# Block rows gathered by token in a routed vision tower, and the second T5 layer's feed-forward split between its units and the choice of experts

## The reference

```python
h = tokens(x)
h = h + spiking_attention(layernorm(h));  h = h + moe8_linear(layernorm(h))       # top 2 of 8
h = h + quant_attention(layernorm(h));    h = h + t5_encoder(layernorm(h))        # 4 layers
h = h + rope_attention(layernorm(h));     h = h + moe16(layernorm(h))             # top 2 of 16
h = h + prope_attention(layernorm(h));    h = h + moe_mixed(layernorm(h))         # top 8 of 16

# t5_encoder, layers 0 to 3: x = x + attn(rms(x)); then layers 0 and 2:
x = x + relu(rms(x) @ wi) @ wo                       # 192 -> 768 -> 192
# and layers 1 and 3 a mixture on y = rms(x):
vals, idx = top_k(y @ gate, 2)                       # 8 experts
x = x + relu(y @ wi) @ wo + sum_e cw_e * gelu(y @ w1_e) @ w2_e
```

## Time and profile before

| | |
|---|---|
| median of 3 runs | 1727.51 us (1727.13 to 1731.24) |
| profiled execution | 1732.31 us, its span 1730.4 us |
| PE busy | 1401.0 us, 81% of the span |
| PEld busy | 1101.9 us, 64% |
| DVE busy | 644.4 us, 37% |
| ACT busy | 467.7 us, 27% |
| POOL busy | 464.5 us, 27% |

### The profile page before, as it was taken

One profiled execution on the slowest core, in us unless ns is written; L12 is line 12 of the kernel. 1 busy time (PEld: TensorE's weight loads), 2 busy tenths in 40 slices (PEclk: granted clock), 3 DMA queues, 4 the chain that ended last, 5 costly groups with the idle time before them and its releaser, 6 DMA issues. The chain is left out here.

```text
span 1730.4 us, 35498 instructions
## 1 busy us (share of the span) xinstructions
PE 1401.0 (81%) x14426; PEld 1101.9 (64%) x14426; DVE 644.4 (37%) x1668; ACT 467.7 (27%) x1226; POOL 464.5 (27%) x597
## 2 busy tenths in 40 slices
PE   6468855999998799599998899668339995876998
PEld 6164433888875798488876589526329993453756
DVE  2445663433432122333342222355511124543424
ACT  0420242443442111243343111123103331422120
POOL 0010273322333243232232424224043441320000
PEclk9688865999998899799999899886559997857999
DMA  5010203100003432600000453240043552020000
GB/s 125 0 29 13 87 1 123 37 2 2 2 3 140 149 114 84 191 2 2 3 2 2 168 183 117 82 118 5 1 171 122 178 187 79 4 57 0 28 27 19
DMA packets 56096, 115.08 MB, mean 67 GB/s; under 512 B 16384, under 2 KB 43268, under 8 KB 50848
## 3 DMA queue, kind: packets, MB, share of 16 engines
q1 hardware_dynamic: 38848, 58.02, 11.3%
q0 software_dynamic: 17088, 54.81, 9.1%
HBM read 137.97 MB, written 24.87 MB: 94 GB/s over the span
## 5 line engine op out<-in xcount | busy, mean ns | idle before, releaser
L1296 PE MATMUL bank<-xT,w 96*128 96x512 f32 x192 | 86.2, 608 | 15.5 <-ACTq L1350 15.5
L1149 PE MATMUL bank<-t_ew,t_hg 128*128 128x192 f32 x552 | 97.2, 327 | 0.0
L1389 DVE SCALAR_TENSOR_TENSOR h<-bank,cw,h 128x192 f32<-128x192 f32 x128 | 53.5, 418 | 99.8 <-PE bank L1312 82.9
L1035 POOL DMA_INDIRECT t_ew<-in_t_moe,source x46 | 48.0, 1043 | 154.8 <-DVE t_og L1217 124.9
L1149 PEld LDWEIGHTS bank<-t_ew,t_hg 128*128 128x128 f32 x552 | 88.7, 190 | 0.2
L329 PE MATMUL bank<-ident,rows 128*96 128x128 f32 x112 | 25.4, 419 | 76.9 <-DVE rows L312 76.9
L1181 ACT ACTIVATE t_hg<-bank 128x384 f32<-128x384 f32 x92 | 40.1, 488 | 168.2 <-PE bank L1137 131.7
L1177 ACT ACTIVATE l_hg<-bank,l_ew 128x128 f32<-128x128 f32 x186 | 51.4, 375 | 122.6 <-PE bank L1137 82.4
L1296 PEld LDWEIGHTS bank<-xT,w 96*128 96x128 f32 x192 | 37.3, 196 | 60.3 <-issue 43.8
L1704 PE MATMUL bank<-t_wo,t_ctx 128*128 128x192 f32 x384 | 75.0, 348 | 0.5 <-ACT t_ctx L1798 0.4
L1133 PE MATMUL bank<-t_xgT,t_ew 128*128 128x128 f32 x552 | 70.8, 279 | 3.8 <-DVE t_xgT L1208 3.3
(11 more groups left out here) (329 smaller groups left out, 3028.3 us busy)
## 6 DMA issues: line engine op xcount, KB each, us to landing
rows_in<-blank SPq DMA_DIRECT2D x2, 2967.0 KB
...
```

What stands on the lines that cost most here:

```text
L1035: pool.indirect_dma_start(k.ew[i % W_SLOTS][:, 0:weights.shape[1]], None, weights, bass.IndirectOffsetOnAxis(ap=k.source[:, b:b + 1], axis=0),
L1149: mm = pe.matmul(k.bank[6 + b % 2][:, 0:DIM], k.hg[b % 2][:, m, :], w[:, SPLIT + m * DIM:SPLIT + (m + 1) * DIM], start=(m == 0), stop=(m = ...
L1296: mm = pe.matmul(k.bank[(u * FC + m) % 4][:], k.w1[s][:, c, m * P:(m + 1) * P], k.xT[:, c, n * HALF:(n + 1) * HALF], start=(c == 0), stop= ...
L1389: ins = dve.scalar_tensor_tensor(out, src, k.cw[:, tile, bass.ds(col, 1)], out, ALU.mult, ALU.add)
```

## The change

- The normed tokens are written to `rows_in` in their own order, by SP, one tile as soon as it is normed: in `t5_pair_phase`, and in `norm_phase` before the 16 experts (`keep`). The two extra columns, `clear_rows` and `send_rows` are gone.
- `plan_blocks` splits each token's place into block and slot, and makes from them 16 one-hot tiles (`hots`) and value tiles (`vals`), which PE multiplies (`list_places`) into a list: which token fills each slot of each block. `keep_list` turns that into `token` (what to gather) and `dest` (where the result goes). Rows are then gathered from `rows_in` by indirect DMAs from POOL (`fetch_rows`), into four slots instead of three; the first four in `fetch_first`, which now also stands in the router phase of the 16 experts.
- The two best experts are picked by two maxima (`choose_two`) instead of a comparison of all pairs; `weigh_two` makes the weights from one Exp of the difference. Top 8 keeps the comparison.
- In `t5_pair_phase` the second layer's units of tiles 0 to 3 do their feed-forward in their steps (w = 8 to 11, `fed` = 12); `t5_choice_phase` is left with tiles 4 to 7.
- The last feed-forward's first layer is split in 128 rows and two halves of 64 rows instead of 96 and 96, and its norm and router with it.

```diff
-X_SLOTS, W_SLOTS, O_SLOTS = 3, 4, 3
-ROW = DIM + REST + 2
-C_TOKEN, C_SECOND = DIM + REST, DIM + REST + 1
+X_SLOTS, W_SLOTS, O_SLOTS = 4, 4, 3
+ROW = DIM + REST
 EXPERT = SPLIT + FC * DIM
...
+            if keep:
+                for t in range(NT):
+                    sp.wait_ge(k.normed, t + 1)
+                    sp.wait_ge(k.doubled, t + 1)
+                    sp.dma_start(k.rows_in[t * P:(t + 1) * P, :], k.rows[:, t, :]).then_inc(k.sent, 16)
+                sp.wait_ge(k.sent, 16 * NT)
...
+                fetch_first(pool, k, nb, sparse)
...
+def choose_two(k, dve, link, n_e, norm, sparse):
+    each = [P, NT, n_e]
+    lg, ex, rest = k.logits[:, :, 0:n_e], k.ex[:, :, 0:n_e], k.cw[:, :, 0:n_e]
+    favour = k.favour[:, 0:n_e].unsqueeze(1).broadcast_to(each)
+    def pick(src, c):
+        best, early, hit = k.red[:, c, :], k.red[:, 4 + c, :], k.picked[:, c, :, 0:n_e]
+        link(dve.tensor_reduce(best, src, AX_X, ALU.max))
+        link(dve.tensor_tensor(hit, src, best.unsqueeze(2).broadcast_to(each), ALU.is_equal))
+        link(dve.tensor_tensor(hit, hit, favour, ALU.mult))
+        link(dve.tensor_reduce(early, hit, AX_X, ALU.max))
+        link(dve.tensor_tensor(k.sel[:, c, :, 0:n_e], hit, early.unsqueeze(2).broadcast_to(each), ALU.is_equal))
+    pick(lg, 0)
+    link(dve.scalar_tensor_tensor(rest, k.sel[:, 0, :, 0:n_e], -BIG, lg, ALU.mult, ALU.add))
+    pick(rest, 1)
     if sparse:
-        dve.wait_ge(k.normed, 1)
-        for c in range(2):
-            link(dve.tensor_tensor(k.picked[:, c, :, 0:n_e], k.sel[:, c, :, 0:n_e], cw, ALU.mult))
-            link(dve.tensor_reduce(k.gate[:, c, :], k.picked[:, c, :, 0:n_e], AX_X, ALU.add))
+        dve.tensor_tensor(k.selb[:, 0:NT * n_e].rearrange("p (t e) -> p t e", e=n_e), k.sel[:, 0, :, 0:n_e],
+                          k.sel[:, 1, :, 0:n_e], ALU.add).then_inc(k.chosen, 1)
+    if norm != "top":
+        link(dve.tensor_tensor(ex, lg, k.red[:, 0, :].unsqueeze(2).broadcast_to(each), ALU.subtract))
+    dve.tensor_tensor(k.gate[:, 1, :], k.red[:, 1, :], k.red[:, 0, :], ALU.subtract).then_inc(k.std_in, 1)
...
+def list_places(pe, k, nb, bank):
+    for i in range(2 * NT):
+        pe.wait_ge(k.slot_known, i + 1)
+        mm = pe.matmul(bank[:, 0:nb], k.hots[:, i, :], k.vals[:, i, 0:nb], start=(i == 0), stop=(i == 2 * NT - 1))
+    mm.then_inc(k.tabled, 1)
...
+    link(dve.tensor_scalar(k.block[:], k.place[:], 1.0 / P, -(P - 1.0) / (2 * P), ALU.mult, ALU.add))
+    link(dve.tensor_scalar(k.block[:], k.block[:], ROUND, None, ALU.add))
+    link(dve.tensor_scalar(k.block[:], k.block[:], -ROUND, None, ALU.add))
+    link(dve.scalar_tensor_tensor(k.slot[:], k.block[:], -float(P), k.place[:], ALU.mult, ALU.add))
+    full = [P, 2 * NT, nb]
+    vals = k.vals[:, :, 0:nb]
+    link(dve.tensor_tensor(vals, k.iota[:, 0:nb].unsqueeze(1).broadcast_to(full),
+                           k.block[:].rearrange("p c t -> p (c t)").unsqueeze(2).broadcast_to(full), ALU.is_equal))
+    link(dve.tensor_tensor(vals, vals, k.home[:].rearrange("p c t -> p (c t)").unsqueeze(2).broadcast_to(full),
+                           ALU.mult))
+    for c in range(2):
+        for t in range(NT):
+            dve.tensor_scalar(k.hots[:, c * NT + t, :], k.iota[:], k.slot[:, c, t:t + 1], None,
+                              ALU.is_equal).then_inc(k.slot_known, 1)
+def keep_list(k, dve, link, nb, bank):
+    choice, none = k.listed[:, 0, 0:nb], k.listed[:, 1, 0:nb]
+    dve.wait_ge(k.tabled, 1)
+    link(dve.tensor_scalar(choice, bank[:, 0:nb], 0.5, -0.75, ALU.mult, ALU.add))
+    link(dve.tensor_scalar(choice, choice, ROUND, None, ALU.add))
+    dve.tensor_scalar(k.token[:, 0:nb], choice, -ROUND, 0.0, ALU.add, ALU.max).then_inc(k.chosen, 1)
+    link(dve.tensor_scalar(none, bank[:, 0:nb], 0.0, SKIP, ALU.is_equal, ALU.mult))
+    link(dve.scalar_tensor_tensor(k.dest[:, 0:nb], bank[:, 0:nb], -1.0, none, ALU.add, ALU.add))
+def fetch_first(pool, k, nb, weights):
+    pool.wait_ge(k.chosen, 2)
+    for i in range(W_SLOTS):
+        fetch_expert(pool, k, i, nb, weights)
+    pool.wait_ge(k.chosen, 3)
+    for i in range(X_SLOTS):
+        fetch_rows(pool, k, i, nb)
+    for i in range(W_SLOTS):
+        pool.wait_ge(k.expert_loaded[i], 16)
+    for i in range(X_SLOTS):
+        pool.wait_ge(k.x_loaded[i], 16)
+    pool.dma_reset(k.sem_range)
...
-def send_rows(pool, k):
-    for c in range(2):
-        for t in range(NT):
-            pool.indirect_dma_start(k.rows_in, bass.IndirectOffsetOnAxis(ap=k.place_i[:, c, t:t + 1], axis=0),
-                                    k.rows[:, t, :], None).then_inc(k.sent, 16)
-    pool.wait_ge(k.sent, 16 * 2 * NT)
+def fetch_rows(pool, k, i, nb):
+    b = sorted_block(i, nb)
+    pool.indirect_dma_start(k.xg[i % X_SLOTS][:], None, k.rows_in,
+                            bass.IndirectOffsetOnAxis(ap=k.token[:, b:b + 1], axis=0)
+                            ).then_inc(k.x_loaded[i % X_SLOTS], 16)
...
+                if b + X_SLOTS < nb:
+                    pool.wait_ge(k.rows_copied, b + 1)
+                    fetch_rows(pool, k, b + X_SLOTS, nb)
...
-        for m in range(FC):
-            g = (r * units + u) * FC + m
-            pe.wait_ge(k.hid_step, g + 1)
-            for c in range(2):
-                mm = pe.matmul(k.bank[(u * FC + m) % 4][:], k.w1[s][:, c, m * P:(m + 1) * P],
-                               k.xT[:, c, n * HALF:(n + 1) * HALF], start=(c == 0), stop=(c == 1))
-            mm.then_inc(k.l1_done, 1)
+        cols = slice(n * HALF, (n + 1) * HALF)
+        for m in range(0, FC, 2):
+            pe.wait_ge(k.hid_step, (r * units + u) * FC + m + 2)
+            pair = [k.bank[(u * FC + m + o) % 4][:] for o in range(2)]
+            for o in range(2):
+                pe.matmul(pair[o], k.w1[s][:, (m + o) * P:(m + o + 1) * P], k.xTs[:, 0, cols], start=True, stop=False)
+            for o in range(2):
+                half = slice(o * REST, (o + 1) * REST)
+                pe.matmul(pair[o], k.w1[s][half, FF + m // 2 * P:FF + (m // 2 + 1) * P], k.xTs[half, 1, cols],
+                          start=False, stop=True).then_inc(k.l1_done, 1)
...
+    fed = NT + NT // 2
...
+            for t in range(NT):
+                sp.wait_ge(k.normed_second, NT + t + 1)
+                sp.wait_ge(k.doubled_second, NT + t + 1)
+                sp.dma_start(k.rows_in[t * P:(t + 1) * P, :], k.rows[:, t, :]).then_inc(k.sent, 16)
+            sp.wait_ge(k.sent, 16 * NT)
...
-                if 0 <= w < NT:
+                if 0 <= w < fed:
                     pe.wait_ge(k.second_kept, w + 1)
-                    features(pairs[0], layer(w).wi, buf.xb[w % 2]).then_inc(k.l1_done, 1)
+                    features(pairs[0], layer(w).wi, turned_second(w)).then_inc(k.l1_done, 1)
...
+            def first(m):
+                cols = slice(HALF, TOK)
+                if m >= 4:
+                    pe.wait_ge(k.hid_step, m - 2)
+                banks = [k.bank[(m + o) % 4][:] for o in range(2)]
                 for o in range(2):
-                    pe.matmul(banks[o], k.w1s[0][:, (m + o) * P:(m + o + 1) * P], k.xTs[:, 0, cols],
+                    pe.matmul(banks[o], k.w1[0][:, (m + o) * P:(m + o + 1) * P], k.xTs[:, 0, cols],
                               start=True, stop=False)
                 for o in range(2):
-                    pe.matmul(banks[o], k.w1s[0][halves[o], FF + m // 2 * P:FF + (m // 2 + 1) * P],
+                    pe.matmul(banks[o], k.w1[0][halves[o], FF + m // 2 * P:FF + (m // 2 + 1) * P],
                               k.xTs[halves[o], 1, cols], start=False, stop=True).then_inc(k.l1_done, 1)
-            def second(n):
-                pe.wait_ge(k.hid_step, (n + 1) * FC)
-                for t in range(4):
-                    i = 4 * n + t
-                    if i >= 4:
-                        pe.wait_ge(k.acc_step, i - 3)
-                    for m in range(FC):
-                        mm = pe.matmul(k.bank[4 + t][:, 0:DIM], k.hT[n][:, m, t * P:(t + 1) * P], k.w2[0][:, m, :],
-                                       start=(m == 0), stop=(m == FC - 1))
-                    mm.then_inc(k.l2_done, 1)
-            first(0, 0)
+            def second(t):
+                pe.wait_ge(k.hid_step, FC)
+                if t >= len(out_banks):
+                    pe.wait_ge(k.acc_step, t + 1 - len(out_banks))
+                for m in range(FC):
+                    mm = pe.matmul(out_banks[t % len(out_banks)][:, 0:DIM], k.hT[0][:, m, t * P:(t + 1) * P],
+                                   k.w2[0][:, m, :], start=(m == 0), stop=(m == FC - 1))
+                mm.then_inc(k.l2_done, 1)
+            first(0)
             pe.wait_ge(k.chosen, 1)
...
-            for i in range(2, 2 * FC, 2):
-                first(i // FC, i % FC)
-            pe.wait_ge(k.chosen, 3)
-            second(0)
-            second(1)
+            count_choices(pe, k, n_e, count_bank, rank_bank)
+            for m in range(2, FC, 2):
+                first(m)
```

(58 more changed lines are left out.)

265 lines of the change are left out of this document (112 added, 153 removed).

## The result

| | before | after |
|---|---|---|
| median | 1727.87 us (1727.13 to 1731.24, 4 runs) | 1701.02 us (1699.40 to 1704.84, 4 runs) |
| ratio | | 0.9838, 95% interval 0.9822 to 0.9855 |
| profiled execution | 1732.31 us, span 1730.4 | 1699.40 us, span 1697.5 |
| PE busy | 1401.0 us | 1402.7 us |
| POOL busy | 464.5 us | 490.2 us |

A forecast was written before the change was run, and what follows sets the result against it. No single engine was taken to bound the kernel; each phase between barriers has its own bound. Terms -5.2 - 18.2 - 11 + 0.3 = -34 us, off the median 1727.5, gave 1693 us, range 1675 to 1715.

The forecast's parts named there:

- Feed-forward in the units: T5 pair phase, steps w = 8 to 11 take on a feed-forward: a loss of 15.1 us a pair, 30.2 for two.
- the end of the units: Last writes of `rows_in` in the T5 pair phase: 0 to 1.5 us could show, taken as 0.
- Choice phase: T5 choice, from its first DVE operation to turn(0): 46.9 us becomes 29.0, gains of 17.9 and 17.5 us.
- The low clock behind it: PE's second layers after the list in the choice phase: one tile at 0.50 takes 4.2 us, three fast ones 6.3.
- the gathers' 560.4: Choice phase: time when gathered rows have landed, weights until 557.3 plus 3.1 us, with turn(0) at 562.1.
- Nearly a wash: T5 feed-forward, both pairs: 30.2 us lost in the units against 35.4 gained in the choices, -5.2 us.
- the block phases: Blocks behind turn(0): still 4.53 us apart, the third POOL call hidden with 0.5 us to spare, 0 us.
- Sixteen experts: Router of 16 experts up to turn(0): shorter choosing, gathers before the barrier, a gain of 18.2 us, bounds 12 and 22.
- Last feed-forward: First layer at the end: 8.9 instead of 10.30 us in each of 8 units, a gain of 11 us.
- B: The three choices end later, by PE holes (1714) or DVE holding POOL's fetches (1703): 1704 to 1722 us, chance 0.25.
- The rule of the Trainium skill: Choices: DVE's 16 `hots` lock POOL out of writing descriptors, 3.2 us in each of three, giving 1703.
- D: POOL bounds the 77 blocks, each 0.1 us a call costing 23 us: above 1722 us, chance 0.08.

The follow-up runs named there:

- x1: The changed kernel once more, unchanged, with a second profile: median 1703.87 us, ratio 0.9839.
- x2: The changed kernel with all eight tiles of the second layer's feed-forward in the choice phase, none in the units: median 1693.95 us, ratio 0.9779.
- x12: x2 once more, unchanged: median 1693.84 us, ratio 0.9806.
- x7: The changed kernel with the 16 experts ranked by the comparison of all pairs, as before: median 1709.81 us.
- x8: The changed kernel with each gather of rows in the block phases issued a second time, into a spare buffer: 1729.3 us, one run.
- x4: The changed kernel with only the last feed-forward undone, 96 + 96 rows again, with its norm and router: median 1710.37 us.

## Why the prediction was right

The sum of the terms came out within 1.1 us of the two profiled executions; each large term did, too.

- **Feed-forward in the units.** 15.2 us a pair against 15.1. The term left at 0, the end of the units, cost 1.7 in both pairs.
- **Choice phase.** 29.25 against 29.0, the last bit by luck. The list was taken to follow DVE; PE paced it, so it ended 17.5 us after the start instead of 15.9, and tokens came 1.4 us later than forecast. The low clock behind it was forecast for one tile of 4.2 us and lasted for one of 4.1; the four tiles took 10.1 us instead of 10.5. What hid the rest of the 1.6 us is that the forecast didn't use its own sum for PE (549 + 10.5 = 559.5) but the gathers' 560.4. PE ended last, 0.4 us behind the last packets. The length of the low clock is itself chance: behind the four lists of the profile after and x1 it was 2.7 to 5.8 us, and turn(0) came after 28.7 to 30.3 us.
- **"Nearly a wash" (-5.2).** The T5 stage got 3.6 to 4.0 us shorter, but less of that than forecast stands where the sum put it: from step w = 8 to turn(0) both pairs together gained 2.5 us in the profile after and 0.5 to 1.8 in the four others. In after and x1 the other 1.3 and 3.2 us lie behind turn(0), in the block phases, a term forecast as 0. And the sum hid two effects of opposite sign. Without the split (x2, x12) the stage is 8 to 10 us shorter than before; the split takes 5 back. It takes 14.9 us out of the first choice (44.1 to 29.25) and puts 15.2 and a longer end into the units. The prediction compared old with new and never worked out the new choice phase with all eight tiles: that step was missing.
- **Sixteen experts.** 17.9 against 18.2; half of it the ranking (x7). Here too errors cancel: `source` came 24.3 us after the norm, 1.7 sooner than forecast (1246.7 - 1220.7 = 26.0), tokens after 36.3, 2.1 later, since a pass of the list took 0.22 us at the low clock. The transfers ended 44.0 us after the norm, for a forecast of 44.2.
- **Last feed-forward.** 11.6 against 11. By the full factor of two that the Trainium skill (TensorEngine Tiling (Array Packing), "Theoretical Speedup") gives as the most, a unit's first layer would be 7.7 us, an estimate. The trace shows 8.9, so the measured pair was the right price.
- **Rivals.** B didn't happen: no hole in PE in any of the choice phases looked at, and POOL's fetches took 1.05 and 1.06 us beside the one-hots, 1.01 without. The rule of the Trainium skill (SBUF — State Buffer, the box on "DVE blocks DMA"), read as the prediction did, for the whole row of one-hots, would have them held for 3.2 us. No run here shows that, only one fetch of 1.26 us among those of the 16 experts. D didn't happen either, and x8 shows that it was priced too high: 4 calls a block cost 27 us, where 0.64 us in each of the 65 blocks would be 42, since the slots' lead absorbs part.
- **The size.** The forecast was 1693, the median 1701.0. Nine runs of the change have a median of 1702.3 us, 48 of the kernel before, over all chips used, one of 1729.2 (1722.9 to 1734.7): -26.9. The profiled execution of before, 1732.31, lies high in that range, the one of after at the low end of its own. I took the sum from one execution and subtracted it from the median of others, and called the difference nothing; between these two profiled executions and the medians it was 6 us. That the moments at which the clock rises make it up is likely, but not shown stage by stage. Which term is smaller than in the profiles stays open: x4 shows 11.4 us in its stage and 6.5 in the medians, x7 9.0 and 7.5.
